# Slot rows gathered by token numbers summed on TensorE, the first slot's rows transposed in their turn, the final sums spread over the slots

## What is computed

```
x = x + tanh(g_xattn) * scan_part(ctx, layernorm(x), ...)
n = layernorm(x)                                   # 2048 tokens x 512
scores = softmax(n @ gate_w.T)                     # 16 experts
topk_w, topk_idx = top_k(scores, 2)
y  = sum over the two experts e of a token: weight * (silu(g) * u) @ w_down[e],  g, u = n @ w_gate_up[e]
y += (silu(gs) * us) @ shared_down                 # one shared expert, twice as wide
x = x + tanh(g_ffn) * y
```

## Time and profile before

| | us |
|---|---|
| median of 3 runs | 1016.52 (1015.74 to 1017.32) |
| the profiled execution, its own time | 1012.7 |
| its span, first to last instruction | 1010.9 |
| PE / DVE / ACT / POOL busy | 891.2 / 738.8 / 593.1 / 571.0 |
| mean granted clock of PE | 0.957 of full |

### The profile page before, as it was taken

How to read it: one execution, slowest core, us unless ns; L and a number is a source line. 1 busy time by engine, 2 the same in 40 slices (tenths; PEclk the granted TensorE clock), 3 DMA queues, 4 the chain that set the end, 5 groups by cost and what they waited for, 6 DMA issues and landing times.

```text
span 1010.9 us, 20635 instructions
## 1 busy us (share of the span) xinstructions
PE 891.2 (88%) x5397; PEld 752.7 (74%) x5397; DVE 738.8 (73%) x1112; ACT 593.1 (59%) x1006; POOL 571.0 (56%) x504
## 2 busy tenths in 40 slices
PE   6898789887988878877999999899999999974796
PEld 3465677566756767766999999899999898863795
DVE  5888989999999999999676676444554554555376
ACT  3669989797989999893332133334544444543121
POOL 5246996888968998987011057232534534531363
PEclk9799979999999999999999999999999999995699
DMA  8106111420115114113111157654657766664476
GB/s 278 44 21 229 33 42 43 154 89 31 53 38 205 42 48 135 44 49 120 42 42 42 53 174 297 213 191 168 232 182 237 238 184 237 227 199 132 139 246 225
DMA packets 65870, 136.39 MB, mean 135 GB/s; under 512 B 8833, under 2 KB 13441, under 8 KB 65666
## 3 DMA queue, kind: packets, MB, share of 16 engines
q1 hardware_dynamic: 54528, 104.68, 31.9%
q0 software_dynamic: 8960, 29.37, 8.1%
q10 hardware_dynamic: 2306, 1.33, 0.6%
HBM read 162.48 MB, written 42.07 MB: 202 GB/s over the span
## 4 chain that ended last, share of the span: by engine, by line
PE 33%; SPq 5%; POOL 5%; issue 5%; ACT 2%; DVE 2%; ACTq 1%; DMA 1%; POOLq 0%; DVEq 0%
PE psY L993 10%; PE psG L957 9%; PE psU L957 9%; POOL slot_in L641 3%; PE psT L950 2%; PE psHT L971 2%; POOL weights L666 1%; SPq L469 1%; SPq L525 1%; SPq L524 1%; ACT weights L1258 1%; SPq L526 1%; SPq L463 1%; SPq L509 1%; DMA xin<-xn_rows 1%
## 5 line engine op out<-in xcount | busy, mean ns | idle before, releaser
L597 POOL TENSOR_TENSOR prod<-hst,cbc 128x512 f32<-128x512 f32 x256 | 327.4, 1312 | 76.6 <-PE y_ps L804 39.5
L1507 DVE TENSOR_TENSOR_SCAN hst<-dA,dbu_ps 128x512 f32<-128x512 f32 x256 | 298.8, 1202 | 20.1 <-issue 10.1
L782 PE MATMUL dbu_ps<-ident,dbuT 128*128 128x128 f32 x1008 | 165.6, 288 | 45.9 <-DVE hst L1507 37.0
L782 PEld LDWEIGHTS dbu_ps<-ident,dbuT 128*128 128x128 f32 x1008 | 115.0, 145 | 107.8 <-DVE hst L1507 68.3
L1305 ACT CAST hh<-psHT 128x384 fp32r<-128x384 f32 x79 | 37.8, 478 | 252.8 <-PE psHT L971 252.8
L1179 ACT ACTIVATE dbuT<-duT,BT 128x512 f32<-128x512 f32 x252 | 160.7, 709 | 17.5 <-PE dbu_ps L782 15.6
L1169 ACT ACTIVATE dA<-dts,Aneg 128x512 f32<-128x512 f32 x256 | 166.4, 709 | 0.2
L804 PE MATMUL y_ps<-ident,prod 128*128 128x128 f32 x1024 | 159.1, 281 | 6.0 <-POOL prod L597 5.3
L957 PE MATMUL psU<-weights,xh 128*128 (+2 forms) x560 | 142.8, 337 | 0.0
L957 PE MATMUL psG<-weights,xh 128*128 (+1 forms) x560 | 137.7, 328 | 4.4 <-DVE xl L1756 3.8
L993 PE MATMUL psY<-weights,hh 128*128 (+3 forms) x420 | 134.1, 400 | 5.7 <-DVE hl L1750 3.3
(11 more groups left out here) (218 smaller groups left out, 1341.7 us busy)
## 6 DMA issues: line engine op xcount, KB each, us to landing
raw_gu<-in_L_ffn_w_gate_up_dram SPq DMA_DIRECT2D x100, 704.0 KB
raw_d<-in_L_ffn_w_down_dram SPq DMA_DIRECT2D x50, 512.0 KB
cbc<-c_rows SPq DMA_DIRECT2D x64, 256.0 KB, 3.2
slot_in<-ztile SPq DMA_DIRECT2D x3, 4096.0 KB, 13.9
gbuf<-slot_in SPq DMA_DIRECT2D x48, 256.0 KB, 3.2
slot_out<-yout POOLq DMA_DIRECT2D x48, 256.0 KB, 3.7
raw_d<-in_L_ffn_w_down_dram SPq DMA_DIRECT2D x50, 192.0 KB
xn_rows<-xin SPq DMA_DIRECT2D x16, 256.0 KB, 2.0
```

The lines of the kernel that those rows point to most:

```text
L597: pool.tensor_tensor(prod[:, prod_slot(n, j), :], hst[:, slot_of(n, j), :], cbc[:, n % 2, :], ALU.mult).then_inc(prod_ready, 1)
L782: last = tr(dbu_ps[j % 2][:, t * P:(t + 1) * P], dbuT[:, n % 2, t, j * P:(j + 1) * P], ident[:])
L1507: V.tensor_tensor_scan(hst[:, slot_of(n, j), :], dA[:, slot_of(n, j), :], dbu_ps[j % 2][:], 0.0, ALU.mult, ALU.add).then_inc(scanned, 1)
```

## The change

The rows no longer travel through slot_in. Instead each slot gets a list of 128 token numbers, and POOL gathers its rows from xn_rows by that list.

- **Lists.** DVE takes each position apart into lane (low 7 bits) and slot (place_parts), marks both as 0/1 in bf16 (lane_marks: 16 tiles x 128 twice; slot_marks: 32 x 48), and multiplies the slot marks by the row's partition number and tile number (id_values). PE sums 32 products of 96 columns into psY[1] (sum_ids, in shared slot 5, before its transposes). DVE turns the sums into integers (slot_tokens, before_result of shared slot 5) and raises ids_ready. Lanes and slots that nobody fills get token 0. combine_weights moves from shared slot 3 to 5. The splits of the first expert's gate weights move from behind slots 4 and 5 to behind 5 and 6, those of its down weights all behind 7.
- **Gathers.** POOL gathers slots 0 to 3 when ids_ready is raised, and slot r + 4 at the head of its round r, ahead of rest_lo(r) and the store; its loop is unrolled. SP's rounds keep only prefetch_expert(r), with no wait for xT_done.
- **First slot.** late is gone: slot 0's rows are transposed and halved where all others' are.
- **End.** The additions follow slots Q1 + 1 to QE - 2 in groups of 1, 2, 3, 2, 2, 3 tiles; tile 13 goes before the result of tile 14's shared part in the last slot, tiles 14 and 15 behind the last h_lo, and the last result is last. For the two last stores SP waits for y_read.
- Gone are the zero fill, ztile, xn_kept_rows and its copies and the waits for them. POOL makes four more constants.

```diff
@@ sync
-                    if n == 5:
-                        sp.dma_start(slot_in[bass.ds(b * ZROWS, ZROWS), :].rearrange("(s p) c -> p s c", p=P),
-                                     ztile[:].unsqueeze(1).broadcast_to([P, ZROWS // P, H])).then_inc(zeroed, 16)
...
-            sp.wait_ge(scattered, 32 * NT)
-            for r in range(4):
-                load_slot(r, r)
...
             with sp.Fori(0, SLOTS // 4 - 1) as m:
                 for k in range(4):
-                    r = m * 4 + k
-                    sp.wait_ge(xT_done, Q0 + r + 1)
-                    load_slot(r + 4, k)
-                    prefetch_expert(r)
+                    prefetch_expert(m * 4 + k)
@@ gpsimd
-            for t in range(NT):
-                for c in range(2):
-                    pool.indirect_dma_start(
-                        slot_in, bass.IndirectOffsetOnAxis(ap=posi[:, c, t:t + 1].bitcast(U32), axis=0),
-                        xn_kept_rows[:, t, :], None).then_inc(scattered, 16)
+            def gather_slot(r, k4):
+                pool.indirect_dma_start(
+                    gbuf[:, k4, :], None, xn_rows,
+                    bass.IndirectOffsetOnAxis(ap=slot_ids[:, r].bitcast(U32), axis=0),
+                ).then_inc(slot_x_ready[k4], 16)
...
+            for k in range(2):
+                pool.wait_ge(xn_stored[k], 16 * (NT // 2))
+            pool.wait_ge(ids_ready, 1)
+            for r in range(4):
+                gather_slot(slice(r, r + 1), r)
...
-            with pool.Fori(0, SLOTS // 2) as m:
-                for k in range(2):
-                    rest_lo(m * 2 + k)
-                    pool.wait_ge(y_read, Q0 + m * 2 + k + 1 + 2)
-                    pool.dma_start(slot_out[bass.ds((m * 2 + k) * P, P), :],
-                                   yout[:, k, :]).then_inc(y_stored[k], 16)
+            for r in range(SLOTS):
+                if r + 4 < SLOTS:
+                    pool.wait_ge(xT_done, Q0 + r + 1)
+                    gather_slot(slice(r + 4, r + 5), r % 4)
+                rest_lo(r)
+                store_slot(r, r % 2)
@@ tensor
+            def sum_ids():
+                pe.wait_ge(id_marks, 1)
+                pe.wait_ge(y_read, NT + 6)
+                for i in range(2 * NT):
+                    last = mm(psY[1][:, 0:2 * SLOTS], in_lane[:, i, :], id_parts[:, i].rearrange("p a s -> p (a s)"),
+                              start=i == 0, stop=i == 2 * NT - 1)
+                last.then_inc(id_sums, 1)
...
+            for n in range(1, NB1 - 2):
+                slot(NT + n, n % 2, 2, 2, loaded(n + 1, (n + 1) % 2), before_transposes=sum_ids if n == 5 else None)
             Q0 = NT + NB1
-            slot(Q0 - 2, 0, 2, 2, loaded(NB1 - 1, 1))
-            slot(Q0 - 1, 1, 2, 2, routed_rows(0, 0), late=True)
+            slot(Q0 - 2, 0, 2, 2, loaded(NB1 - 1, 1), before_down=ids_read)
+            slot(Q0 - 1, 1, 2, 2, routed_rows(0, 0))
@@ vector
+            def lane_marks(i):
+                V.tensor_tensor(in_lane[:, i:i + NT], iota_l[:].unsqueeze(1).broadcast_to([P, NT, P]),
+                                pos_b[:, 0, i:i + NT].unsqueeze(2).broadcast_to([P, NT, P]), ALU.is_equal)
...
+            def id_values():
+                V.tensor_scalar(id_parts[:, :, 0], in_slot[:], iota_p[:], None, ALU.mult)
+                V.tensor_tensor(id_parts[:, :, 1], in_slot[:],
+                                iota_t[:].rearrange("p c t -> p (c t)").unsqueeze(2).broadcast_to([P, 2 * NT, SLOTS]),
+                                ALU.mult).then_inc(id_marks, 1)
...
+            shares = {1: tables_and_places, 2: order_and_lanes, 3: lanes_and_slots, 4: id_values, 5: combine_weights}
...
+            slot(Q1 + 1, 1, "shared", NB1)
+            add_tiles(0)
+            slot(Q1 + 2, 0, "shared", NB1 + 1)
+            add_tiles(1, 2)
+            slot(Q1 + 3, 1, "shared", NB1 + 2)
+            add_tiles(3, 4, 5)
+            for n in range(4, NB1 - 2):
+                slot(Q1 + n, n % 2, "shared", NB1 + n - 1)
+                add_tiles(2 * n - 2, 2 * n - 1)
             slot(QE - 2, 0, "shared", NT - 3)
+            add_tiles(2 * NB1 - 6, 2 * NB1 - 5, 2 * NB1 - 4)
+            slot(QE - 1, 1, "shared", NT - 2, last_slot=True, before_result=last_of_pair6)
             h_lo(QE - 1, 1)
+            add_routed(2 * NB1 - 2, 2, NB1 - 1)
+            add_routed(2 * NB1 - 1, 3, NT - 1)
+            dve.wait_ge(f_added, 2 * NB1)
             result_to(QE - 1, 1, "shared", NT - 1)
```

190 lines of the change are left out of this document (105 added, 85 removed).

## The result

| | us | granted clock |
|---|---|---|
| before, median of 4 runs | 1016.92 (1015.74 to 1020.25) | |
| changed, median of 4 runs | 1002.65 (997.99 to 1003.92) | 0.960 to 0.972 |
| ratio | 0.9852, 95% interval 0.9824 to 0.9881 | |
| changed, its profiled run | 1003.06, span 1001.3 | 0.960 |

The change is worth 14.3 us. The prediction was 1010.0, 7.4 us too high, and its range ended at 1004.5, so the range missed too. The two profiled spans differ by 9.6 us only (1010.9 and 1001.3): the profiled run of before (1012.7) lay 4 us under its median, that of the changed kernel lies at its median.

What follows compares the result with a forecast made beforehand. PE was taken as the bound for nearly all of 480 to 1000 us, except in two places. Front +0.7 and shared tail -7.3 gave -6.6 us: a median near 1010, range 1004.5 to 1017.

Steps and rivals of the forecast that it cites:

- 32 matmuls: Sums of slot numbers on PE before shared slot 5's transposes: 2.9 us of cost at 0.09 each, 1.4 to 3.4 possible.
- used slots: From the second routed slot to the last used one PE is full, so no gain: 0.
- the carrying over: Differences summed on the profiled execution (1012.7 us) were applied unchanged to the timed median, 3.8 us above it.
- SP's rounds, and the slots behind them: Slots without tokens and shared tiles behind: rounds fall from 4.48 to 3.5 us, saving 2.2 and 6.7, together -8.9.
- First slot's rows in their turn: End of the shared slots: slot 0's product starts 3.2 us earlier and at full clock, 1.5 more: 4.7 saved.
- Marks on DVE: Shared slots 2 and 3: lane marks of 2.3 us each delay PE by 2.5 us, bounds 1.6 to 2.9.
- Final sums: Shared tail: 1.6 us lost to gathers, 2.6 to two groups of three tiles, 2.7 saved at the end.
- Rival 1: Empty slots wait for their gathers: median 1016.5 at a 6.9 us landing; chance 0.07 up to 1016.5, 0.10 beyond.
- Rival 2: PE's 2.2 us idle in shared slot 2 brings half clock, +1.9 us; with upper bounds median 1014; chance 0.12.
- Rival 3: SP's rounds keep 4.48 us and the third shared tile's wait remains: 1016 us; chance 0.06.
- Rival 4: Marks and sums at lower bounds, gathers landing in 3.4 us: another 4 us gained, median 1005.5; chance 0.13.
- Taking the scatters out at 0: Removing the 32 scatters was given no term of gain; copies and zeros were taken at 0, up to 0.5 possible.

Runs made afterwards that it cites:

- SP relieved: Kernel before, with only the routed slots' loads moved from SP to POOL as plain transfers: 1037.8 us, ratio 0.9915 to before of its group.
- scatters back: Changed kernel with 32 scatters of zeros into an unread tensor put back: 1032.3 us (0.9846) in group 4, 1009.5 us (0.9939) in group 2.
- group 4: Follow-up runs timed together, kernel before at 1049.2 us; the changed kernel took 1014.1 us, ratio 0.9666.
- group 2: Follow-up runs timed together, kernel before at 1016.6 us; the changed kernel took 1003.1 us, ratio 0.9876.
- groups 2 and 3: Two groups of follow-up runs, with the kernel before at 1016.6 us and at 1048.9 us.
- Before again: Kernel before, unchanged, run once more for a second trace: 1046.9 us, ratio 0.9993 to before of its group.

## Why the prediction was off, point by point

The prediction was 7.4 us too high. 3.0 of them are in the traces, which differ by -9.6 where the sum had -6.6, and 4.3 in carrying that difference over to the median. Neither part alone leaves the range: with the traces' -9.6 the prediction would have been 1006.9, with the sum as it was and the 4.3 about 1005.7. The steps that failed are the 32 matmuls, priced at 2.9 us and measured at 1.39, the used slots, taken at nothing and measured at -1.54, and the carrying over. The scan part, +0.94 by chance, hides a part of it.

- **SP's rounds, and the slots behind them: right, and in its size partly by luck.** -8.85 us against -8.9: 2.2 in the empty slots for 2.2, and 6.7 up to the fourth shared tile for 6.7 (the parts written down add up to 6.5). The rounds are 3.75 us and not 3.5, still under the 4.0 allowed, and 0.54 us of the third tile's wait stayed. But the first trace of before has the longest such stretch of its kind, 73.3 us; seven others take 71.4 to 72.7, and eleven of changed kernels 63.9 to 65.6, so 7 to 8 us is the usual gain. "SP relieved" shows the term by itself, 6.6 us.
- **First slot's rows in their turn: right.** The way from the last shared item's transposes to the second routed slot's is 18.17 us before and 13.41 after, 4.76 less for 4.7.
- **Marks on DVE: right.** PE is 2.27 us later, 2.08 in shared slot 3 and 0.19 behind it, for 2.5. The lane marks take 2.27 us, the rate of f32. The Trainium skill, Vector Engine (DVE) Microarchitecture Reference, section 5.1, says so of a 2-byte instruction one of whose two sources repeats an element; by that rule, the trace agrees, and the one-source multiplication of 1536 elements at 0.61 us, against 1.75 for the two-source one, shows the other side.
- **32 matmuls: mis-sized.** 1.39 us on PE, predicted 2.9. "The weight load stays whole" was wrong: 43 ns each is what the columns alone were to take, my lower bound. The 0.4 us for y_read did not come. This makes 1.5 and the marks 0.2 of the 1.8 us by which the front came out under +0.7.
- **Used slots: the step was missing.** "PE is full there, so a us elsewhere is worth nothing" held for the slots as they average, not for those where an expert begins. The 1.54 us lie mostly in slots between 18 and 35 which take 7.1 to 7.7 us in before instead of 6.7, up to 0.63 us in one. "SP relieved" has the gain too (2.2), so it comes from the slot loads that left SP. Which wait it goes through isn't shown: from 640 to 895 us POOL's waits for ACT fall from 42.9 to 18.3 us, ACT's for raw_gu from 36.5 in ten to 31.5 in nine, so hardly each.
- **Final sums: a near sum of terms that missed.** +0.94 for +1.5. DVE waits 1.61 us for the first tile, as predicted, but PE does not lose 1.6: wait and two additions take as long as the four additions that stood there in before, and the item is 0.17 us longer. The groups of three cost PE 1.14 and 1.49 us, 2.6 as predicted. The end behind the last h_lo is 1.5 us shorter and not 2.7, by a wait of 1.28 us for the last tile's gathers that the sum didn't have.
- **Rival 1 did not come.** The gathers of one repeated row land in 3.8 to 5.3 us. The period of the empty slots stayed 3.78 us.
- **Rival 2 did not come.** Behind PE's idle of 1.86 us the granted clock from 600 to 610 us is 1.00.
- **Rival 3 did not come.** SP's rounds fell from 4.48 to 3.75 us.
- **Rival 4 was the right direction**, for a part of its reasons: the 32 matmuls at their lower bound, not the marks or the landing.
- **"I carry differences over" is the largest miss.** The range took its ends from terms of one trace. It had no term for before's own executions, whose first three runs lay 3.8 us over the profiled one. A profiled run outside the timed runs' range is no picture of the median: either it was fast by chance, or the median holds something that the trace does not and that the change may take out. Here it was worth 4.3 us, mostly by chance as far as the traces tell. At the other level the second case is shown: before has a stop of 27 us that the changed kernel lacks, and the gain is 35 us, 21 more than at the level of the result.
- **Taking the scatters out at 0** was right in the stretch beside them, where PE is full in the trace of before, and wrong at the other level. It is the part whose worth depends most on the level: 18.2 us by "scatters back" in group 4, 6.4 in group 2. The 6.4 come from the first gathers standing behind the scatters, as before's slot loads do; the prediction books that way under the first slot's rows.

## What to carry to other kernels

When one engine walks ahead of the others through rounds of reads and skipped transfers, count its period against theirs; moving one transfer with its wait to another queue was worth most of this change in the traces. Where the profiled run lies outside the timed runs, widen the range by the distance on the side where the removed work lies. And lay several traces of the same kernel side by side before calling a term of 1 us right: the same stretch differed by up to 2 us between traces of one kernel, the scan part by more than 6. A long row of indirect transfers is not free because PE is full beside it in one trace: time it in several groups of runs before taking it at nothing.

## What the runs showed of the hardware

- **Engines stop beside long rows of POOL's indirect transfers, at one of two levels.** 27 to 29 us beside 32 scatters in seven traces of before and of kernels that differ from it elsewhere, 13 us in another kernel with as many, 5 to 12 us beside 32 gathers in the final sums; nothing at the other level with the same instructions. The level was the same for all runs of a group, and differed between groups 2 and 3, which the record gives the same chip.
- **What they wait for is not in the trace.** The traces record transfers of code for two queues. From 604 to 636 us the changed kernel of group 4 has three packets of them:

```profile
q8 instruction: 2, 0.03, 0.6%
q14 instruction: 1, 0.01, 0.1%
```

  "Before again" has none in that stretch, and 1700 packets of POOL's queue. In the first trace of before one comes near 607 and one near 625 us; in "before again" none comes between 594 and 636. The Trainium skill, Runtime: NRT & Kernel Launch, section "Instruction fetch mechanics", says that each engine fetches its code by its own transfers and that this is mostly hidden. A code transfer that waits behind POOL's would look like these stops; but stopped engines ask for no code either, so the rows do not decide it, and no run here shows it.
- **Two-source work on POOL held up DVE's two-source work:** 4.43 us for 1.10.
- **32 matmuls of 96 bf16 columns, each with a weight load of its own, ran at 43 ns from start to start.**
- **Gathers of 128 descriptors that all read one row** landed like any others, 4.0 us.
